# Sampling by base values and clipped steps of column differences, with a rearranged prologue and the base cells summed by GpSimd

## The reference

```python
offsets = _conv2d(x, off_w, off_b)              # 8 heads x 9 taps x (x, y)
aw = jax.nn.sigmoid(_conv2d(x, attn_w, attn_b)) # one weight per head and tap
gx = gx_base + off[:, :, :, 0] * (2.0 / W)
xp = (gx + 1.0) * 0.5 * (W - 1)                 # likewise yp
x0 = jnp.floor(xp); wx1 = xp - x0
sampled = corner(y0, x0, wy0 * wx0) + corner(y0, x1, wy0 * wx1) + \
          corner(y1, x0, wy1 * wx0) + corner(y1, x1, wy1 * wx1)
head_out = jnp.einsum('nhckxy,nhkxy->nhcxy', sampled, awr)
return jnp.einsum('oc,nchw->nohw', Wo, combined)
...
x = x + _L0_conv_ref(_gn(x), ...)
x = x + _L1_conv_ref(_gn(x), ...)
```

## Time and profile before

| | |
|---|---|
| median of three runs | 149.56 us |
| the profiled execution, its own time | 150.8 us |
| its span, first to last instruction | 148.9 us |
| PE, DVE, ACT, POOL busy | 130.4, 111.5, 59.2, 18.6 us |
| chain that ended last, shares | PE 51%, DVE 24%, issue 9%, ACT 5%, DMA 4%, POOL 2% |
| mean granted clock of PE | 0.966 |

### The profile page before, as it was taken

One profiled execution on the slowest core, in us unless ns is written; L12 is line 12 of the kernel. 1 busy time (PEld: TensorE's weight loads), 2 busy tenths in 40 slices (PEclk: granted clock), 3 DMA queues, 4 the chain that ended last, 5 costly groups with the idle time before them and its releaser, 6 DMA issues.

```text
span 148.9 us, 3277 instructions
## 1 busy us (share of the span) xinstructions
PE 130.4 (88%) x1390; PEld 111.0 (75%) x1390; DVE 111.5 (75%) x207; ACT 59.2 (40%) x108; POOL 18.6 (13%) x27
## 2 busy tenths in 40 slices
PE   4991899998997999999999998899779999797790
PEld 3771899996997989999899986787445567465460
DVE  5579991493489997999979999998574297965701
ACT  3069569639904494036942046001120317021100
POOL 8940600000000000000054000000011001030100
PEclk9999659999999999999999999999995999999999
DMA  2920000049843000000000000000000000000033
GB/s 87 232 31 0 0 0 4 0 141 256 186 108 72 2 4 0 0 0 4 0 0 0 4 0 0 0 0 4 2 0 4 0 4 4 0 4 0 0 75 70
DMA packets 6624, 4.85 MB, mean 33 GB/s; under 512 B 4672, under 2 KB 5954, under 8 KB 6610
## 3 DMA queue, kind: packets, MB, share of 16 engines
q1 hardware_dynamic: 6002, 4.12, 11.3%
q10 hardware_dynamic: 608, 0.52, 1.4%
HBM read 2.22 MB, written 0.52 MB: 18 GB/s over the span
## 4 chain that ended last, share of the span: by engine, by line
PE 51%; DVE 24%; issue 9%; ACT 5%; DMA 4%; POOL 2%; SPq 1%; POOLq 1%; DVEq 0%
PE bank L979 11%; PE bank L998 9%; PE bank L1023 7%; DVE prod L739 7%; PE bank L971 6%; DMA prod<-in_w_off 4%; PE bank L1120 4%; DVE part L766 3%; DVE x_t L858 3%; PE bank L1153 3%; PE bank L948 2%; DVE wy L774 2%; DVE pooled L864 2%; DVE bn L586 2%; PE bank L932 2%
## 5 line engine op out<-in xcount | busy, mean ns | idle before, releaser
L739 DVE TENSOR_TENSOR prod<-hat,wy 128x1440 f32<-128x1440 f32 (+3 forms) x25 | 27.3, 1158 | 0.0
L766 DVE TENSOR_TENSOR part<-v,bank 128x1280 f32<-128x1280 f32 (+3 forms) x20 | 21.7, 1109 | 7.0 <-PE bank L1023 3.5
L998 PE MATMUL bank<-cst,prod 128*128 128x128 f32 (+3 forms) x189 | 22.3, 272 | 0.8 <-DVE prod L739 0.8
L1023 PE MATMUL bank<-cst,part 128*128 128x128 f32 x168 | 21.1, 274 | 1.8 <-DVE part L766 1.4
L998 PEld LDWEIGHTS bank<-cst,prod 128*128 128x128 f32 (+3 forms) x189 | 20.7, 131 | 1.4 <-DVE prod L739 1.0
L979 PE MATMUL bank<-w_cross,g_cross 128*128 128x216 f32 x144 | 21.0, 296 | 0.5 <-POOL bias_r L385 0.5
L1023 PEld LDWEIGHTS bank<-cst,part 128*128 128x128 f32 x168 | 18.3, 140 | 3.2 <-DVE part L766 3.0
L979 PEld LDWEIGHTS bank<-w_cross,g_cross 128*128 128x128 f32 x144 | 19.6, 213 | 0.6 <-issue 0.6
L932 PE MATMUL bank<-ones_r 128*128 128x512 f32 x62 | 17.5, 433 | 2.1 <-POOL w_pair L370 2.1
L971 PE MATMUL bank<-w_pair,g_pair 128*128 128x216 f32 x96 | 14.6, 292 | 3.4 <-ACT g_cross L432 3.4
L932 PEld LDWEIGHTS bank<-ones_r 128*128 128x128 f32 x62 | 12.4, 209 | 4.7 <-POOL w_pair L370 2.1
(11 more groups left out here) (94 smaller groups left out, 159.3 us busy)
## 6 DMA issues: line engine op xcount, KB each, us to landing
v<-v SPq DMA_DIRECT2D x2, 480.0 KB, 6.1
v<-v SPq DMA_DIRECT2D x2, 448.0 KB, 5.8
prod<-in_w_off SPq DMA_DIRECT2D x1, 486.0 KB, 5.7
w_s<-in_w SPq DMA_DIRECT2D x4, 72.0 KB, 4.1
wc_s<-in_wc SPq DMA_DIRECT2D x2, 144.0 KB, 2.9
wp_s<-in_wp SPq DMA_DIRECT2D x4, 72.0 KB, 2.4
...
```

Of the source, the lines that this page charges most:

```text
L739: return nc.vector.tensor_tensor(prod[:, 0:K2 * CELLS * cx].rearrange("p (k q s) -> p q k s", k=K2, s=cx)[:, q0:q0 + nd], hat[:, c % 2, d0 ...
L766: nc.vector.tensor_tensor(part[:, n % PARTS, 0:nd, 0:cv].rearrange("p d (q e) -> p d q e", e=HD), moved, weights.unsqueeze(3).to_broadcast ...
L998: last = nc.tensor.matmul(out_ps[0:size, b * P:(b + 1) * P], prod[:, at:at + size], ident, start=(b == 0 and t == 0), stop=(b == n - 1 and ...
L1023: last = nc.tensor.matmul(comb_bank[:, j * P:(j + 1) * P], part[:, n % PARTS, d, j * P:(j + 1) * P], ident, start=(m == 0 and d == 0 and j ...
```

## The change

The interpolation along x is written in another form. In a row, value at p = v(base) + sum over k of clip(p - k, 0, 1) * (v(k+1) - v(k)), where base is the leftmost column of the window. So each row has one base cell and 4 (outer rows 2) steps; a step's weight is a clipped function of x times the base weight, and it multiplies the column difference `dv`. There are again 21 cells: 16 steps and 5 bases. A base weight is hat(y) * mod alone, needs no product, and is written straight into `prod`; the products are 16 cells instead of 21. The nine taps of the 16 steps are summed by PE in two groups of 8 cells instead of three; those of the 5 bases by POOL in four additions. The bases are applied last, in one instruction. SP shifts v and dv together, in two pieces of columns, in eight DMAs.

In the prologue ACT writes zeros into dv, makes both parts of `w_pair`, and casts directly from `g_t` instead of from `g_pair`; the bias moves from POOL to DVE and ahead; `w_cross`'s low part is made in two pieces; range 2 is normalised by DVE alone; PE waits by column and apart for pair and cross taps; the values are made in two halves; 26 warm-up matmuls instead of 16; POOL no longer works between its first power and the end of the ranges. r12 and maxima lie in `vd` instead of `x_t`.

```diff
-GROUPS = ((0, 8, 2), (8, 15, 3), (15, 18, 4))
...
+GROUPS = ((0, 8, 2), (8, 16, 5))
+APPLY = ((0,), (1,), (2,), (3, 4))
+TERMS = (4, 4, 4, 4, 5)
+VCOLS = W + 3
+PIECES = (0, 5, VCOLS)
+RANGES = ((0, 5), (5, 10), (10, PW))
+DVE_IMAGES = (N, N // 2, N)
+LOW_TAPS = (0, 5, K2)
...
-WARM_LOAD, WARM_START, WARM_CHUNK = 11, 16, (0, 0, 0, 16, 10)
+WARM_LOAD, WARM_START, WARM_CHUNK = 11, 26, (0, 0, 0, 16, 10)
...
+        def base_sums(c, engine, queue):
...
+            taps = prod[:, 0:K2 * CELLS * cx].rearrange("p (k s) -> p k s", k=K2)[:, :, BASE0 * cx:CELLS * cx]
+            done = 4 * c
+            engine.tensor_tensor(taps[:, 0:4], taps[:, 0:4], taps[:, 4:8], ALU.add).then_inc(base_steps, 1)
+            queue.wait_ge(base_steps, done + 1)
+            engine.tensor_tensor(taps[:, 0:2], taps[:, 0:2], taps[:, 2:4], ALU.add).then_inc(base_steps, 1)
+            queue.wait_ge(base_steps, done + 2)
+            engine.tensor_tensor(taps[:, 0], taps[:, 0], taps[:, 1], ALU.add).then_inc(base_steps, 1)
+            queue.wait_ge(base_steps, done + 3)
+            engine.tensor_tensor(cell[:, :, 0:cx], taps[:, 0].rearrange("p (q s) -> p q s", s=cx),
+                                 taps[:, 8].rearrange("p (q s) -> p q s", s=cx), ALU.add).then_inc(base_steps, 1)
...
+            for k, copied in enumerate((1, 4)):
+                sp.wait_ge(v_ready, copied)
+                sp.wait_ge(dv_ready, k + 1)
+                for i in range(1, ND):
+                    dst, src = row_parts(i)
+                    at = BASES[i] - BASES[0]
+                    xa, xb = max(PIECES[k], at), PIECES[k + 1]
+                    sp.dma_start(vd[dst, i, :, xa - at:xb - at, :], vd[src, 0, :, xa:xb, :]).then_inc(moved[k][i], 16)
...
+            pool.wait_ge(g_low, len(RANGES))
             nc.gpsimd.memset(wp_s[:, :, :, :], 0.0).then_inc(wp_zero, 1)
...
+            for k, copied in enumerate((1, 4)):
+                xa, xb = PIECES[k], min(PIECES[k + 1], VCOLS - 1)
+                pool.wait_ge(v_ready, copied)
+                nc.gpsimd.tensor_tensor(dv[:, 0, xa:xb, :], v[:, 0, xa + 1:xb + 1, :], v[:, 0, xa:xb, :],
+                                        ALU.subtract).then_inc(dv_ready, 1)
+            for c in range(NC):
+                pool.wait_ge(prod_ready, ND * (c + 1))
+                if c:
+                    pool.wait_ge(part_ready, ND * c)
+                base_sums(c, nc.gpsimd, pool)
+                if c == NC - 2:
+                    borders_and_mask()
...
-                act.wait_ge(g_high, r + 1)
+                act.wait_ge(g_normed, r + 1)
...
-                nc.scalar.activation(g_pair[hi, xl - 1:xb - 1], g_pair[lo, xl:xb], ACT.Copy)
-                nc.scalar.activation(g_cross[hi, xa:xb], g_pair[lo, xa:xb], ACT.Copy).then_inc(g_copied, 1)
-
+                nc.scalar.activation(g_pair[hi, xl - 1:xb - 1], g_t[:, xl:xb], ACT.Copy).then_inc(g_shifted, 1)
+                nc.scalar.activation(g_cross[hi, xa:xb], g_t[:, xa:xb], ACT.Copy).then_inc(g_copied, 1)
...
-                q0 = CELL0[OWN_ROW]
-                own_sum = tick(nc.vector.tensor_reduce(
...
+                for m, rows in enumerate(APPLY):
+                    if c and m == 2:
                         residual(c - 1)
-                    apply(i)
+                    apply_steps(rows)
...
+                apply_bases()
...
+            for half in range(2):
+                for j in range(2 * half, 2 * half + 2):
+                    conv_column(1, j)
+                values(half)
+            pe.wait_ge(v_ready, 4)
...
                 tap_sum(c, 0)
-                tap_sum(c, 1)
-                cells_back(c, 0)
-                tap_sum(c, 2)
-                cells_back(c, 1)
-                cells_back(c, 2)
                 if c:
                     y0(c - 1)
+                cells_back(c, 0)
+                tap_sum(c, 1)
+                cells_back(c, 1)
```

365 lines of the change are left out of this document (199 added, 166 removed).

## The result

The changed kernel takes 142.81 us (median of 4 runs, 142.34 to 144.95) where the kernel before, on the same chip, takes 149.33 (median of 4, 149.03 to 150.86). The ratio is 0.953, with a 95% interval of 0.945 to 0.962: faster, by some 7 us. The forecast was 143.1.

The account below looks back on a forecast made before the run. The start-up chain was taken to bound the first 37 us, PE chunks 1 and 2, DVE chunk 3. A start-up gain of 3.0 us grows to 6.5 at the last residual; 149.56 less that gives 143.1, range 140.8 to 147.3.

Parts of the forecast that it names:

- First column: Start-up: PE starts its first convolution column at 13.5 us, with no idle before it and full clock; before, 14.52.
- The rival that the waits of chunk 0 bring the clock down: PE's idle in chunk 0 lowers its clock, 1.7 to 3.3 us an episode, 144.8 to 146.4 us; chance 0.20.
- Images of the second range: Start-up: DVE's four images of the second range take 1.1 us, or 2.2 by the disturbed row.
- Chunk 0's waits: PE idles 1.0 and 0.6 us behind ACT in chunk 0; first column of chunk 2 at 33.8, 3.0 gained.
- DVE's work: Fewer products and the reduction given to POOL: 3.2 us less per four-column chunk, half in short ones, 12.8 in all.
- Chunks 1 and 2: PE bounds them; they take 17.65 and 18.0 us, so chunk 2 starts at 61.5 and chunk 3 at 79.5.
- Chunk 3: DVE sets the pace; it takes 13.5 us, so chunk 4 starts at 93.0, 5.6 ahead.
- POOL's sums: Four additions per chunk take 3.6 us, hidden; rival that POOL is late: 147.3 at the upper bound, halfway 145.2, chance 0.12.
- POOL slows DVE: Base sums beside DVE's row applications cost chunk 3 1.5 us and chunk 4 0.8, giving 145.4; chance 0.06.
- The row shifts: The second set, issued at 31.7, lands at 50.3 to 52.5; chunk 1 asks at 52.4: hidden, 0 to 2 us spare.
- The rival "slower": Second shift lands more than 6.5 us behind 52.4, making the kernel slower; 157.7 us at 0.1 MB/us; chance 0.02.
- more than forecast: Tail: the clock's fall near 112 us does not recur, 1.7 us less, 141.4; chance 0.10.

Follow-up runs that it names:

- e1: The changed kernel with 16 start-up warm-up matmuls instead of 26; 143.30 us, ratio to the kernel before 0.965.
- e3: The kernel before with only the new prologue, sampling untouched and values in one piece; 152.17 us, ratio 1.023.
- e6: The changed kernel with POOL's memset of wp_s placed beside DVE's images of the second range; 143.19 us, ratio 0.964.
- e2: The changed kernel with the base cells summed by one DVE reduction per chunk instead of POOL's four additions; 143.87 us, ratio 0.970.
- e4: The changed kernel with row sums placed ahead of the convolution columns in chunks 0 to 2; 141.76 us, ratio 0.954.
- e5: The changed kernel with five more unused POOL additions of 256 elements per chunk, except the last; 142.76 us, ratio 0.961.
- e7: The changed kernel with the second block's weight loads issued ahead of the second set of row shifts; 143.02 us, ratio 0.959.
- e8: The changed kernel with column work moved into PE's waits for ACT's copies and row sums ahead of the next columns; 140.23 us, ratio 0.940.
- e11: e8 with the second set of row shifts cut in two, columns 5 to 8 first; 140.00 us, ratio 0.942.
- e9: e3 with the values' matmuls in two halves, each behind two columns of chunk 1; 148.58 us, ratio 0.998.
- e10: e3 with six warm-up matmuls on PE ahead of the value matmuls; 147.49 us, ratio 0.993.

## Why the prediction was right, and where its steps were off

The sum held: 6.63 us gained at the last residual where 6.5 were forecast, and 142.81 against 143.1. The mechanism is the forecast one. That the figures agree within 0.1 is in part luck: the tap sums of chunk 1 came 0.3 late, chunk 2 was 0.3 shorter than forecast, and with the other start-ups seen for the same code (tap sums of chunk 0 from 29.52 to 30.84, the chunks as in after) the gain would have been 6.0 to 7.4. By its steps:

- **First column** at 13.95, not 13.5, with the clock at full. The step (no idle before the first column) was right, and one term of it mis-sized: the bias load, which I gave 0 to 0.4 us and took as 0, since DVE's low part of w_cross would be last. The bias now stands ahead on ACT and on DVE too, and both waited for it (rows of ACT and of DVE in after):

```profile
8.91 0.39 ACT L471 ACTIVATE bias_r<-bias_s 128x216 fp32r<-128x216 f32 x1 [1.06 <-DMA bias_s<-in_off_bias]
```
```profile
9.40 0.38 DVE L790 TENSOR_TENSOR bias_r<-bias_s,bias_r 1x216 fp32r<-1x216 f32 x1 [0.92 <-ACT bias_r L471]
```

  DVE begins the images of the first range at 10.58 instead of 10.14, and ACT ends the shifted copy at 13.80 instead of the forecast 13.4. The warm-ups themselves ended as late, because the clock rose late in this run (see the last section).
- **The clock's price was spread wider than I gave, and its risk lay in the wrong place.** I gave an episode 1.7 to 3.3 us. One at the start (e1) cost 0.7 to 1.5, as part of it lay on a wait, and one in the tail 1.4 to 1.7. The rival that the waits of chunk 0 bring the clock down did not come. But e3 showed one that I had not looked for: 1.42 us of idle ahead of the values, and 4.9 us gone. The whole change avoids it through values in halves. I had read that edit as a matter of PE's order only and priced it at nothing.
- **Images of the second range** took 1.05 us (forecast 1.1, other bound 2.2). e6 shows the cause that I inferred from two rows.
- **Chunk 0's waits**: 0.86 and 0.37 us of idle around the second tap sum, forecast 1.0 and 0.6. First column of chunk 2 at 34.09 for 33.8: the 0.45 of the start, less what these waits gave back.
- **DVE's work** shrank as forecast: products and reductions took 28.9 + 6.9 us before and 23.0 after, 12.8 less.
- **Chunks 1 and 2** took 17.65 and 17.70 for 17.65 and 18.0. The wait of 0.65 between the groups was 0.47, and ACT's offsets did not lengthen chunk 2 by the 0.25 that I added. That PE bounds them, so that most of DVE's 12.8 us are worth nothing, is what e2 and e4 show: reduction back on DVE, no change there.
- **Chunk 3** took 13.43 for 13.5, and chunk 4 7.75 for 7.8. Here DVE sets the pace. e2 puts 1.63 us on a reduction there, but on one of 1440 elements and 2.72 us; the 1.694 of the earlier trace rows is for 864. What leaving out that smaller one brought by itself was not measured.
- **POOL's sums** took 3.7 us a chunk for 3.6. They come to 2.1 ns per element and 0.2 us fixed. The Trainium skill, page "GPSIMD Engine Reference", section on elementwise accounting, gives 4497 ns for 2048 elements, 2.2 ns each; the trace agrees, and the estimate of 2.8 us per chunk from it fell short for want of the fixed part and of the gaps between the four. The upper bound, 6.9 ns from one partition's row, was far off.
- **POOL slows DVE**: the applications with weights in PSUM kept their 1.22 us beside POOL's work (e5), so this rival was void where it mattered. It holds for other instructions (below). The "42% longer" in it is the share of the slowed time that was lost; 0.445 for 0.26 us is 71% longer, and e6 measured 59%.
- **The row shifts** were the weak step. I had the last land at 50.3 to 52.5. The second set went out from 32.31; its issue on SP's queue was itself held up, the last went out at 36.7, took 16.5 us, and landed at 53.2, 0.3 before DVE asked at 53.5. That is 3.25 MB in 20.9 us, 0.16 MB/us: the plain rate of before was the right one, and the higher one, with 2 us taken off, was not. The right price for being late is not one for one as I wrote, since DVE has slack there: a wait of 1.73 us cost nothing in e4, and 1.00 nothing in e7. With PE's own waits filled (e8, e11) 1.67 cost 0.3. The rival "slower" stood further off than I put it.
- **The tail** gave 1.4 us in the profiled run. It is chance. A fall of 6.8 us at half clock, as at the start of before, lowers the mean clock to 0.977, and the two falls of its trace to 0.966. Of 19 runs of before that ran beside e9 to e11, four had a mean clock of 0.966, as in the profiled run with its two falls, and took 150.6 to 151.0. Ten others had 0.976 or 0.977 and took 148.3 to 149.7. The ten runs of e10 part in the same way: 147.15 to 147.64 at 0.997 to 1.0, 148.75 to 149.01 at 0.988. By such medians a fall in the tail costs 1.5 to 2 us. That the mean clock sorts the times is not always so: in e9 the runs at 0.988 took 147.87 to 149.50 and those at 1.0 took 147.72 to 149.33. So a part of the scatter, the start-up's for one, has nothing to do with this fall. My rival "more than forecast" treated it as a property of the kernel.

What stays open: why the tail's clock falls in some executions and not in others, why the clock rises so differently at the start, and why the fall in e1 ended after 3.4 us and those in e3 and in before lasted longer. Nor does a run part the new sampling's 3.95 us further: the nine transposes, the two groups in place of three and the place of y0 were changed together.
